# Three float32r products in place of fp32 in a Mamba layer's C and out projections, with LayerNorm statistics in halves, a new order of one FFN part and single buffers

## The reference, cut to what matters

```python
x = x + 0.5 * ffn(layernorm(x))          # part A
x = x + ssm(layernorm(x))                # part B
x = x + 0.5 * ffn(layernorm(x))          # part C

# ffn(x): h = silu(x @ wg.T) * (x @ wu.T); return h @ wd.T      (768 hidden, weights int / 127)
# ssm(x):
xz = x @ in_proj_w.T; x_in, z = split(xz)                        # 512 + 512 channels
xc = causal_conv(x_in, 4 taps) + conv_b
dt_r, Bm, _ = split(xc @ x_proj_w.T)
delta = clip(softplus(dt_r @ dt_proj_w.T + dt_proj_b), 0.001, 0.1)
A_bar = exp(delta * A); B_bar = (A_bar - 1) / A * Bm             # A = -exp(A_log), 128 states
h[t] = A_bar[t] * h[t-1] + B_bar[t]                              # scan along the sequence
y = h @ C_proj_w.T + xc * D
return (y * silu(z)) @ out_proj_w.T
```

## Time and profile before

| | |
|---|---|
| runs of the kernel | 532.61, 534.18, 535.38 us (median 534.18) |
| the profiled execution, span | 532.8 us |
| mean granted TensorE clock | 0.980 |
| PE busy | 501.4 us, 94% |
| DVE busy | 414.6 us, 78% |
| ACT busy | 280.0 us, 53% |
| POOL busy | 227.5 us, 43% |

### The profile page before, as it was taken

How to read it: one execution, slowest core, us unless ns; L and a number is a source line. 1 busy time by engine, 2 the same in 40 slices (tenths; PEclk the granted TensorE clock), 3 DMA queues, 4 the chain that set the end, 5 groups by cost and what they waited for, 6 DMA issues and landing times.

```text
span 532.8 us, 7720 instructions
## 1 busy us (share of the span) xinstructions
PE 501.4 (94%) x2657; PEld 294.7 (55%) x2657; DVE 414.6 (78%) x865; ACT 280.0 (53%) x472; POOL 227.5 (43%) x192
## 2 busy tenths in 40 slices
PE   2789988999999999999999999999999999998696
PEld 2446436646484557546574557546674648545444
DVE  4788997897869976997889876997789876877332
ACT  5383961477408771577318660677328760673032
POOL 1132237154733736063823646172814555083122
PEclk9898999999999999999999999999999999999869
DMA  8401000002020022003110112002100200000001
GB/s 297 123 0 43 1 0 2 0 2 42 22 60 2 11 31 80 1 2 42 40 41 1 24 19 80 1 2 42 51 29 2 41 22 21 1 1 22 20 1 41
DMA packets 27240, 16.84 MB, mean 32 GB/s; under 512 B 15264, under 2 KB 26528, under 8 KB 27184
## 3 DMA queue, kind: packets, MB, share of 16 engines
q1 hardware_dynamic: 26368, 15.26, 10.9%
q10 hardware_dynamic: 816, 0.79, 0.5%
HBM read 8.71 MB, written 4.19 MB: 24 GB/s over the span
## 4 chain that ended last, share of the span: by engine, by line
PE 82%; DVE 8%; ACT 3%; issue 3%; DMA 1%; POOL 1%; POOLq 0%; SPq 0%; DVEq 0%; ACTq 0%
PE q L1567 53%; PE dp L1567 25%; PE tp L1472 3%; DVE xc L956 1%; DMA hh<-in_L_ffn_w_gate_dram 1%; DVE h L931 1%; POOL hl L426 1%; ACT xc L557 1%; DVE wmx L1051 0%; DVE rmx L1092 0%; DVE xn L899 0%; DVE ser L988 0%; DVE x L942 0%; ACT sg L581 0%; PE q L1472 0%
## 5 line engine op out<-in xcount | busy, mean ns | idle before, releaser
L426 POOL TENSOR_TENSOR hl<-h,hh 128x512 f16<-128x512 f32 x96 | 121.9, 1284 | 103.1 <-ACT hh L589 103.0
L931 DVE SCALAR_TENSOR_TENSOR h<-sg,hsm,q 128x512 f32<-128x512 f32 x96 | 70.6, 742 | 34.5 <-PE q L1567 22.2
L956 DVE SCALAR_TENSOR_TENSOR xc<-xi,cw,xc 128x512 f32<-128x512 f32 x96 | 84.8, 898 | 0.5
L563 ACT ACTIVATE xh<-tp 128x512 f16<-128x512 f32 x36 | 19.7, 598 | 118.0 <-PE tp L1472 118.0
L581 ACT ACTIVATE sg<-q 128x512 f32<-128x512 f32 x96 | 56.7, 591 | 37.2 <-PE q L1567 37.2
L589 ACT ACTIVATE hh<-h 128x512 f16<-128x512 f32 x96 | 60.1, 628 | 27.5 <-DVE h L931 27.3
L433 POOL TENSOR_TENSOR xcl<-xc,xch 128x512 f16<-128x512 f32 x32 | 40.8, 1284 | 49.2 <-ACT xch L614 49.2
L1567 PE MATMUL dp<-wo,yu 128*128 128x256 f32 x256 | 60.2, 388 | 1.5 <-POOL yu L441 1.5
L1567 PE MATMUL dp<-wd,hl 128*128 128x256 bf16 x384 | 53.4, 275 | 1.7 <-POOL hl L426 1.7
L1567 PE MATMUL dp<-wd,hh 128*128 128x256 bf16 x384 | 53.7, 276 | 1.0 <-ACT hh L589 0.9
L1567 PEld LDWEIGHTS dp<-wo,yu 128*128 128x128 f32 x256 | 48.4, 195 | 9.6 <-POOL yu L441 2.7
(11 more groups left out here) (184 smaller groups left out, 847.5 us busy)
## 6 DMA issues: line engine op xcount, KB each, us to landing
xpre<-in_L_attn_x_dram SPq DMA_DIRECT2D x8, 512.0 KB, 4.5
out_dram<-x SPq DMA_DIRECT2D x16, 256.0 KB, 2.1
xc<-in_L_attn_in_proj_w_dram SPq DMA_DIRECT2D x1, 1024.0 KB, 11.0
hl<-in_L_ffn_w_up_dram ACTq DMA_DIRECT2D x3, 256.0 KB, 5.7
hh<-in_L_ffn_w_gate_dram SPq DMA_DIRECT2D x3, 256.0 KB, 6.5
hh<-in_L_ffn_w_down_dram SPq DMA_DIRECT2D x1, 768.0 KB, 8.0
yu<-n_L_attn_out_proj_w_dram SPq DMA_DIRECT2D x1, 512.0 KB, 5.0
yu<-in_L_attn_x_proj_w_dram SPq DMA_DIRECT2D x1, 256.0 KB, 11.3
```

Of the source, the lines that this page charges most:

```text
L426: pool.tensor_tensor(HL[g.f][:, c, :], H[:, j, :], HH[g.f][:, c, :], ALU.subtract)\
L563: act.activation(XH[g.f][:, kc, :], tp[kc][:, :], ACT.Copy, scale=XS).then_inc(t_hi[kc], 1)
L931: dve.scalar_tensor_tensor(out=H[:, first % 3, :], in0=SG[:, first % 2, :], scalar=HSM[:, c:c + 1], in1=q[bank][:, :], op0=ALU.mult, op1=A ...
L956: dve.scalar_tensor_tensor(out=XC[s][:, m, :], in0=XI[s][:, m, k:k + TILE], scalar=CW[:, m, k:k + 1], in1=XC[s][:, m, :], op0=ALU.mult, op ...
```

## The change

Eight things change together.

- The C and out projections take float32r operands, each split into a rounded high part and the rest: high x high, low x high and high x low, three products for one. The weights are split once, on POOL, at the start (`wide_weights`).
- After the scan DVE makes the two parts of the states (`state_split`). After the gating, ACT makes the high part of `YU` (`high_y`) and DVE the low part (`low_y`).
- In PE's order, `cp0` and `cp1` move forward between gate and up products of A, `cp2` and `cp3` stay behind them; `turn0` of the next LayerNorm moves ahead of `out10`, `turn1` behind it.
- On DVE the scan, undivided and with `state_split`, comes before the first `hidden` of A; the `skip_y`, `low_y` and residuals of C are spread between the `hidden` of A; `delta_in` precedes both `split_lo`.
- On ACT `input_in` moves ahead of the second table load, and the high parts of `YU` are spread between the gates of A.
- On POOL the first two gatings move between the low halves of A.
- `variance` works on two blocks at a time with `bn_aggr`, and `root` on two blocks; `normalize` waits for each pair.
- `HH`, `HL`, `SZ`, `YU` and `HS` have one buffer. Weights in natural layout lie in other tiles at the start.

```diff
@@ ORDER
-         ("up1", "A"), ("gate2", "A"), ("up2", "A"), ("gate3", "A"), ("up3", "A"), ("gate4", "A"),
-         ("up4", "A"), ("gate5", "A"), ("up5", "A"), ("cp0", "B"), ("cp1", "B"), ("cp2", "B"), ("cp3", "B"),
+         ("up1", "A"), ("cp0", "B"), ("gate2", "A"), ("up2", "A"), ("cp1", "B"), ("gate3", "A"), ("up3", "A"),
+         ("gate4", "A"), ("up4", "A"), ("gate5", "A"), ("up5", "A"), ("cp2", "B"), ("cp3", "B"),
          ("down00", "A"), ("down01", "A"), ("down10", "A"), ("down11", "A"), ("out00", "B"), ("out01", "B"),
-         ("out10", "B"), ("turn0", "Bnext"), ("turn1", "Bnext"), ("out11", "B"))
+         ("turn0", "Bnext"), ("out10", "B"), ("turn1", "Bnext"), ("out11", "B"))
@@ POOL
+            def wide_weights(n):
...
+                pool.tensor_copy(high, whole).then_inc(wide_hi, 1)
+                pool.wait_ge(wide_hi, n + 1)
+                pool.tensor_tensor(low, whole, high.bitcast(F32), ALU.subtract).then_inc(wide_lo, 1)
...
-                    hidden_low(g, "A", (0, 1, 2, 3, 4, 5))
-                if B:
-                    gate_y(g, (0, 1, 2, 3))
+                    hidden_low(g, "A", (0,))
+                if B:
+                    gate_y(g, (0,))
                 if A:
-                    root(g, "Bnext")
+                    hidden_low(g, "A", (1,))
+                if B:
+                    gate_y(g, (1,))
+                if A:
+                    hidden_low(g, "A", (2, 3, 4, 5))
+                if B:
+                    gate_y(g, (2, 3))
+                if A:
+                    root(g, "Bnext", 0)
+                    root(g, "Bnext", 1)
...
-            conv_low(start, (0, 1, 2, 3))
+            wide_weights(0)
+            wide_weights(1)
+            conv_low(start, (0, 1))
+            wide_weights(2)
+            conv_low(start, (2, 3))
@@ ACT
+            def high_y(g, chunks):
+
+                for m in chunks:
+                    act.wait_ge(yu_ready, IC * g.index() + m + 1)
+                    act.activation(YUH[:, m, :], YU[:, m, :], ACT.Copy).then_inc(yuh_ready, 1)
...
                     decay_exp(g)
+                    input_in(g)
                     table(ACT.Silu, 4)
...
+                    hidden_high(g, "A", (2,))
+                if B:
+                    high_y(g, (0,))
                 if A:
...
+                    gate(g, "A", (4,))
+                    hidden_high(g, "A", (3,))
+                if B:
+                    high_y(g, (1,))
+                if A:
+                    gate(g, "A", (5,))
+                    hidden_high(g, "A", (4,))
+                    hidden_high(g, "A", (5,))
+                if B:
+                    high_y(g, (2, 3))
@@ DVE
+            def variance(g, k, parts=(0, 1)):
+
+                for part in parts:
+                    dve.wait_ge(st_ready[k], 2 * g.turn(k) + part + 1)
+                    for b in (2 * part, 2 * part + 1):
+                        ins = dve.bn_aggr(MV[k][:, b, :], ST[k][:, b, :])
+                    ins.then_inc(mv_ready[k], 1)
+                    dve.wait_ge(mv_ready[k], 2 * g.turn(k) + part + 1)
+                    blocks = slice(2 * part, 2 * part + 2)
+                    dve.tensor_scalar(VE[k][:, blocks], MV[k][:, blocks, 1], EPS, None, ALU.add)\
+                        .then_inc(ve_ready[k], 1)
...
+            def state_split(g):
+
+                dve.wait_ge(hs_ready, g.index(1))
+                dve.tensor_copy(HSH[:, :], HS[:, :]).then_inc(hsh_ready, 1)
+                dve.wait_ge(hsh_ready, g.index(1))
+                dve.tensor_tensor(HSL[:, :], HS[:, :], HSH[:, :].bitcast(F32), ALU.subtract).then_inc(hsl_ready, 1)
+
+            def low_y(g, chunks):
+
+                for m in chunks:
+                    dve.wait_ge(yuh_ready, IC * g.index() + m + 1)
+                    dve.tensor_tensor(YUL[:, m, :], YU[:, m, :], YUH[:, m, :].bitcast(F32), ALU.subtract)\
+                        .then_inc(yul_ready, 1)
...
                     delta(g)
                     series(g, (0, 1, 2, 3))
-                if A and g.h > 0:
-                    hidden(g, "A", (0, 1))
-                if B:
                     decay_out(g)
                     input_out(g)
-                if A:
-                    hidden(g, "A", (2, 3))
-                if B:
                     halo(g)
                     scan(g)
+                    state_split(g)
+                if A and g.h > 0:
+                    hidden(g, "A", (0,))
                 if C:
                     residual(g, "C", 0)
-                if A:
-                    hidden(g, "A", (4, 5))
-                if B:
-                    skip_y(g, (0, 1, 2, 3))
+                if A and g.h > 0:
+                    hidden(g, "A", (1,))
+                if B:
+                    skip_y(g, (0,))
                 if C:
                     residual(g, "C", 1)
                 if A:
+                    hidden(g, "A", (2,))
+                if B:
+                    skip_y(g, (1,))
+                if A:
+                    hidden(g, "A", (3,))
+                if A:
+                    hidden(g, "A", (4,))
+                if B:
+                    low_y(g, (0,))
+                if A:
+                    hidden(g, "A", (5,))
+                if B:
+                    skip_y(g, (2, 3))
+                    low_y(g, (1,))
+                if A:
                     residual(g, "A", 0)
-                    stats(g, "Bnext", (0,))
+                if B:
+                    low_y(g, (2,))
+                if A:
+                    stats(g, "Bnext", (0, 1))
+                    variance(g, "Bnext", (0,))
+                if B:
+                    low_y(g, (3,))
+                if A:
                     residual(g, "A", 1)
-                    stats(g, "Bnext", (1, 2, 3))
-                    variance(g, "Bnext")
+                    stats(g, "Bnext", (2, 3))
+                    variance(g, "Bnext", (1,))
                     normalize(g, "Bnext", (0, 1, 2, 3))
@@ PE
+                product(g, f"cp{m}", "B", [(WCH[:, cols], HSH[:, :]), (WCL[:, cols], HSH[:, :]),
+                                           (WCH[:, cols], HSL[:, :])],
+                        waits={2: (hsl_ready, g.index(1))} if m == 0 else {})
...
+                onto_tokens(g, "B", j, [(YUH, m, w) for m in range(IC) for w in (WOH, WOL)] +
+                            [(YUL, m, WOH) for m in range(IC)], blocks=blocks,
+                            waits={2 * m: (yuh_ready, IC * g.index() + m + 1) for m in range(IC)} |
+                                  {2 * IC + m: (yul_ready, IC * g.index() + m + 1) for m in range(IC)})
```

More of the change, by code:

```diff
@@ L44 @@
 U32 = mybir.dt.uint32
+F32R = mybir.dt.float32r
 ALU = mybir.AluOpType
@@ L163, in number, with turn @@
         return NUMBER[family, part, self.h - back] + more
+    def turn(self, kind):
+        return self.h - 1 if kind == "C" else self.h + 1
     def index(self, more=0):
@@ L476, in _ @@
             hidden_low(before, "A", (1, 2, 3, 4, 5))
-            root(before, "Bnext")
-            conv_low(start, (0, 1, 2, 3))
+            root(before, "Bnext", 0)
+            root(before, "Bnext", 1)
+            wide_weights(0)
[3 more added lines that the diff above has]
+            conv_low(start, (2, 3))
             hidden_low(start, "A", (0, 1, 2, 3, 4, 5))
             gate_y(start, (0, 1, 2, 3))
-            root(start, "Bnext")
+            root(start, "Bnext", 0)
+            root(start, "Bnext", 1)
             for h in range(1, LAST - 1):
                 half(Half(h))
-            root(late, "C")
+            root(late, "C", 0)
+            root(late, "C", 1)
             conv_low(late, (0,))
@@ L491, in _ @@
             gate_y(late, (0, 1, 2, 3))
-            root(last, "C")
+            root(last, "C", 0)
+            root(last, "C", 1)
             hidden_low(last, "C", (0, 1, 2, 3, 4, 5))
@@ L539, in fill @@
                 else:
-                    act.activation(WO[:, 2 * j:2 * j + 2, :], pair, ACT.Copy).then_inc(w_act, 1)
+                    act.activation(WO[j][:, :], bank[:, :], ACT.Copy).then_inc(w_act, 1)
             def copy_rank():
@@ L620, in silu_z @@
                     act.wait_ge(q_full[bank], uses)
-                    act.activation(SZ[g.b][:, m, :], q[bank][:, :], ACT.Silu,
+                    act.activation(SZ[:, m, :], q[bank][:, :], ACT.Silu,
                                    scale=RIV[:, IC + m:IC + m + 1]).then_inc(sz_ready, 1)
@@ L804, in _ @@
             hidden_high(start, "A", (4, 5))
+            high_y(start, (0, 1, 2, 3))
             norm_hi(start, "Bnext", (0, 1))
@@ L841, in _ @@
             input_in(late)
+            high_y(late, (0, 1, 2, 3))
             norm_hi(last, "C", (0, 1))
@@ L1330, in half @@
                     stats(ahead, "A", (1,))
-                if ahead.has("C"):
-                    stats(ahead, "C", (0, 1))
             before, start, late, last = Half(-1), Half(0), Half(LAST - 1), Half(LAST)
@@ L1405, in _ @@
             scan(start)
```

(10 more changed lines are left out.)

165 lines of the change are left out of this document (87 added, 78 removed).

## The result

The changed kernel takes 546.01 us (median of 4 runs, 544.66 to 546.97) where the kernel before, on the same chip, takes 533.39 (531.43 to 535.38): 1.0232 times as long, with a 95% interval of 1.0204 to 1.026.

A forecast was written before the change was run, and what follows sets the result against it. PE was taken to bound the six halves. Waits of 3.1 us less 2.1 saved gave 1.0 a half, 6.0 over six; start +2.0, end -1.4: +6.6 on 532.8, with 1.4 to the median 540.8 us; range 527 to 553.

The forecast's parts named there:

- Price of a product: PE, C and out projections: float32r products at 0.216 (512 columns) and 0.117 us (256), saving 2.1 us a half.
- Rival 3: Out projection: loads of 0.195 us bind, 557 us; with two passes near 575; chance 0.11.
- PE's new wait at cp0: At cp0 and gate2 of each half: PE waits for scan, state split and hidden 0; 1.2 us taken.
- The low halves and POOL: First down block of each half: POOL's last low half comes late through gatings and locks; PE idle 0.9 us.
- Out projection and turn: End of each half: PE waits 0.8 us at turn0 for the LayerNorm, and 0.2 after the last turn.
- Start: Before half 1: weight pieces under the taps, split, new links and products saved, together +2 us.
- ahead of hidden 4 and 5 (1.1): At the start: the state split on DVE ahead of hidden 4 and 5 costs 1.1 us.
- the two new links before out00 (0.7 beyond its other terms): At the start: two new links ahead of the out projection cost 0.7 us beyond its other terms.
- End: Where C and out lie bare: 3.3 less for products, copy 0.5 and high_y and low_y 1.4 on top: -1.4 us.
- 3.3 less: Behind the last gating: some 37 instructions of 0.117, 4.3 us, replace 26 taking 7.57 us, 3.3 less.
- Parts at nothing: Parts priced at no time: statistics in halves, ACT's high_y and moved input_in, single buffers, second transposing DMA, moved residual C1.
- Statistics in halves: LayerNorm: two aggregates and one addition per block pair replace seven tiny steps for four; POOL's root twice; worth nothing.

The follow-up runs named there:

- e5: Changed kernel with cp0 and cp1 two products later in the six middle halves, hidden 0 of A ahead of the scan, hidden 1 ahead of the state split: 543.07 us.
- e7: Kernel before with the new order of the A part, the statistics in halves and the single buffers, both projections in fp32: 531.66 us.
- e2: Changed kernel without POOL's six weight-split pieces at the start; rounded weights used twice in place of the low halves: 543.15 us.
- e8: Changed kernel with the out projection back in fp32 from YU itself, C still three float32r products: 539.27 us.
- e4: Kernel before with the LayerNorm statistics in halves alone, nothing else of the change: 529.61 us, 0.9931 of the kernel before.
- e9: Changed kernel with later cp0, cp1 and turn0, fourth gating on DVE, low_y 0 ahead of hidden 5, fp32 projections in first and last half: 526.75 us.
- e10: Combined version e9 with cp2 ahead of gate5, hidden piece 5's terms last in two down blocks, POOL's second gating and norm_lo earlier: 525.68 us.
- e3: Changed kernel with the C projection in fp32 from the scan's output at its new place, no state split, out still float32r: 532.74 us.

## Why the prediction was right, and where it was not

The case forecast came (slower; 546.0 in 527 to 553, and in the forecast's own 537 to 550), by the mechanism named for the halves; the start was mis-sized, the end right only in its sum. The loss is 12.6 us where 6.6 were added up, and of the 6.0 between them 5.4 are the start. By the prediction's own sign (a start more than 4 us longer) the loss was put in the wrong place there; that the time still lies in the range is owed to the range's width.

- **Price of a product: right.** 0.1185 at 256 columns (0.117 taken) and 0.232 at 512 (0.216): out takes 48x0.1185 = 5.69 us instead of 6.91, C 12x0.232 = 2.78 instead of 3.43, so 1.9 us are saved a half instead of 2.1. Rival 3 is out.
- **PE's new wait at cp0: right.** 1.2 was taken; e5, with the same instructions and no wait there, comes to the down block 1.24 us earlier. By e7, some 0.2 of it comes with the order even in fp32.
- **The low halves and POOL: right.** 0.9 taken; 12 terms of 0.109 take 1.31, the rows give 272.86 to 275.23, 1.06 lost. low_y takes 1.65 in that half's first case and 1.08 on average, beside POOL.
- **Out projection and turn: near.** 0.8 taken; 0.49 in the row, 0.66 from the start of out01's last product (281.92) to turn0 (282.70) less the product's own 0.12. The 0.2 at iz0 didn't show.
- **The half: 60.05 against 60.2, 5.6 us over six against 6.0.** The prediction did not price the order for itself; e7 puts it at 0.5 of what it called waits. Two errors nearly cancel: the saving is 0.2 smaller than taken, and the statistics, put at nothing, give 0.33.
- **Start: +2 taken, +7.4 measured.** The taps (2.5 taken) were right: 2.7 by e2. Wrong was the split "ahead of hidden 4 and 5 (1.1)": it falls beside POOL's hl and takes 2.74, of which 1.7 comes through in e8 (moving it away from there was not tried by itself). Wrong were "the two new links before out00 (0.7 beyond its other terms)" with the out products' saving of 1.3 set against them: four low halves, 3.48 us, stand in the chain there, and that stretch is 1.2 longer than in e7, not shorter. And the prediction has no clock in it: where PE waits for the split, the level falls in the change, and C's products and the first down terms lie in stretches at 0.61 and 0.50. Two executions of the same start (the change and e5) differ by 2.2 us, 0.9 of it already ahead of the first tap and 1.3 between the scan and the last skip_y; from 89.9 to 92.5 the clock is at 0.50 in the one and at 0.99 in the other. What makes it fall is open: e8 has the same split, and there it stays up.
- **End: -1.4 taken, -0.6 measured, right by chance.** Here "3.3 less" failed. The bare products take 6.80 us instead of 7.58, 0.8 less, the first of them at the lower clock (0.50 from 509.2 to 512.7):

```profile
509.22 6.80 PE dp L1670 x42
```

  They begin 2.4 us later in the half than before (1.9 taken): gating beside low_y takes 5.95 us over four pieces instead of 4.95. So they end 1.6 later, where 1.4 earlier was forecast. What turns the sum is the statistics, put at nothing: their shorter chain puts the first normalization 51.3 us behind half 7's begin, 51.4 before. Against e7, which has that chain and fp32 products, the end is 3.6 longer (78.5 and 74.9).
- **Parts at nothing: "Statistics in halves" failed.** The run with them alone is 3.8 us faster (e4). The step looked for their cover in the halves, where 0.33 each shows through, and not at the end, where the LayerNorm stands bare and 1.7 can be read off; what the clock adds there in e4 is not shown to be theirs. The single buffers were not run by themselves; the other parts of that list cost nothing that the traces show.

The Trainium skill (TensorE: Matmul & The Clock Gate, LDWEIGHTS) gives a weight load as its columns over 1.2 GHz, so 107 ns, and by it the estimate of the saving was 2.5 us. The trace does not agree: one out product follows the other at 0.1185 us and 1.9 us are saved, nearer to the 0.117 of the transposes in the kernel before.

## What to carry to other kernels

Work taken from the engine that is the bound is worth its time only if the work that prepares it fits the queues of the others: here 1.9 us of TensorE a half was paid with six pieces on VectorE, five of which stand ahead of what TensorE waits for: two at cp0, one ahead of hidden 5, two ahead of the normalization at the turn. Beside GpSimd they grow (low_y to 1.08 us on average), and so do GpSimd's gatings (1.40 instead of 1.27). When such a wait is removed by a change of order, look at once for the next queue that ends there; e5, e9 and e10 each moved it. And price every part at the beginning and the end of the kernel on their own: a step that is hidden in the loop can be bare there, as the statistics were.

## What was not expected of the hardware

The load of a float32r weight tile lasts as long as the fp32 one but does not set the pace: the next follows at 0.1185. The row among the groups by shape:

```profile
L1670 PEld LDWEIGHTS dp<-woh,yul 128*128 128x128 f32 x128 | 18.2, 196 | 0.4 <-DVE yul L1091 0.4
```

What DVE and POOL cost each other is large. Alone and beside the other engine, hsh takes 0.43 and 1.20, hsl 0.69 and 1.54, a tap 0.76 and 1.69, low_y 0.68 and 1.65, POOL's pieces 1.16 and 1.6. Whether pieces meet depends on their place: with two or four weight pieces at the start (e8, e3) the twelve taps take 11.0 and 11.4 us, with none (e2) 11.0, with all six 13.7.

The granted clock went to its lower level (1.2 GHz, 0.50 in the rows) behind stretches in which PE had waited, and there the same 26 products at the end took 7.58 us instead of 5.89. What decides is open: ahead of those products PE was busy 2.56 of 4 us in the kernel before, where the clock fell, and 2.51 in e4, where it did not.
